# Transformer layer with attention and a mixture of experts on one core: the eight experts as one block, indirect transfers one at a time, and extra products ahead of the routing step

## The reference, cut to what matters

```python
xn = layernorm(x)                                   # x: 8 batches x 512 tokens x 128 channels
x  = x + attention(xn) + moe(xn)
# attention: 16 heads of width 8, keys where xn[..., 0] == 0 are masked
scores = einsum('bthd,bshd->bhts', q, k) * 8 ** -0.5;  attn = softmax(scores)
out    = einsum('bhts,bshd->bthd', attn, v) @ wo.T + bo
# moe: 8 experts, each of the 4096 tokens goes to its top 2, at most 1280 tokens an expert
logits = xt @ gate_w;  top_logits, top_idx = top_k(logits, 2)
rank   = cumsum(one_hot(top_idx)) - 1;  keep = rank < 1280
h      = gelu(exp_batches @ c_fc + fc_bias)         # exp_batches: 8 x 1280 x 128, h: 8 x 1280 x 512
y      = h @ c_proj + proj_bias
out    = sum over the two experts of weight * y[expert, rank]
```

## Time and profile before

| | us |
|---|---|
| median of 3 runs | 838.06 (835.35 to 841.63) |
| the profiled execution | 828.99 |
| its span, first to last instruction | 826.8 |
| PE busy | 614.4 (74%) |
| DVE busy | 410.8 (50%) |
| ACT busy | 403.2 (49%) |
| POOL busy | 220.1 (27%) |
| mean granted TensorE clock | 0.812 of full |

### The profile page before, as it was taken

The page is one execution under the profiler, slowest core; times in us unless marked ns, Lnnn a source line. Parts: engine busy times, 40 slices in busy tenths (PEclk is TensorE's granted clock), DMA queues, the critical chain, the costliest instruction groups (busy, mean ns, idle before and its releaser), DMA issues.

```text
span 826.8 us, 9722 instructions
## 1 busy us (share of the span) xinstructions
PE 614.4 (74%) x3502; PEld 306.7 (37%) x3502; DVE 410.8 (50%) x617; ACT 403.2 (49%) x781; POOL 220.1 (27%) x222
## 2 busy tenths in 40 slices
PE   5648997101399999899989999999989510269985
PEld 3423322000133333693358535863477100022322
DVE  6758676000278888317841685158713210045742
ACT  3340365000267777637883578457745200135761
POOL 3865128777200002000010002000200777740000
PEclk9975578555579999999999999999999655555975
DMA  7883341111101014112411232111312211100011
GB/s 199 254 261 115 128 160 61 51 51 51 39 22 41 28 35 131 33 33 73 122 41 33 69 95 73 33 53 48 104 44 72 72 51 51 50 22 22 2 52 51
DMA packets 57999, 60.44 MB, mean 73 GB/s; under 512 B 8032, under 2 KB 42848, under 8 KB 57952
## 3 DMA queue, kind: packets, MB, share of 16 engines
q1 hardware_dynamic: 52160, 45.92, 18.3%
q0 software_dynamic: 5792, 13.90, 5.4%
HBM read 29.65 MB, written 29.62 MB: 72 GB/s over the span
## 4 chain that ended last, share of the span: by engine, by line
PE 52%; another core or an unknown queue 13%; DVE 13%; ACT 10%; issue 6%; SPq 3%; DMA 3%; DVEq 0%; ACTq 0%
PE bX L933 14%; PE bPV L949 14%; PE bD L1039 9%; DVE nmax L731 8%; ACT probs L585 5%; PE bD L914 4%; ACT hid L615 2%; PE bX L923 2%; DMA k_rows<-hid 2%; PE bPV L1072 2%; PE bX L1024 2%; PE bX L1028 1%; PE bX L1025 1%; PE bD L968 1%
## 5 line engine op out<-in xcount | busy, mean ns | idle before, releaser
L731 DVE TENSOR_REDUCE nmax<-bD 128x2 f32<-128x1024 f32 x256 | 301.1, 1219 | 226.4 <-remote 147.7
L585 ACT ACTIVATE probs<-bX 128x512 f32<-128x512 f32 x512 | 269.4, 597 | 249.0 <-PE bX L933 110.0
L933 PE MATMUL bX<-Q,K 27*128 27x512 f32 x512 | 196.6, 519 | 133.4 <-issue 98.8
L933 PEld LDWEIGHTS bX<-Q,K 27*128 27x128 f32 x512 | 79.2, 202 | 291.0 <-issue 146.9
L949 PE MATMUL bPV<-probs,v_aug 128*32 128x512 f32 x1024 | 158.1, 693 | 1.6 <-ACT probs L585 0.7
L914 PE MATMUL bD<-K,Q 25*128 25x512 f32 x512 | 143.5, 529 | 14.8 <-issue 4.7
L487 POOL TENSOR_TENSOR wfc_hi<-wfc,ones 128x512 fp32r<-128x512 f32 x8 | 10.2, 1275 | 355.2 <-DMA pjb<-in_pjb 355.2
L1039 PE MATMUL bD<-wpj,hid 128*128 128x128 f32 x640 | 74.0, 276 | 7.7 <-DVE xeT_lo L764 4.8
L914 PEld LDWEIGHTS bD<-K,Q 25*128 25x128 f32 x512 | 60.7, 206 | 50.3 <-DVE nmax L731 23.3
L1039 PEld LDWEIGHTS bD<-wpj,hid 128*128 128x128 f32 x640 | 72.4, 192 | 9.4 <-issue 9.4
L615 ACT ACTIVATE hid<-bX,fcb 128x512 f32<-128x512 f32 (+1 forms) x96 | 55.2, 615 | 27.4 <-PE bX L1028 26.6
(11 more groups left out here) (103 smaller groups left out, 462.6 us busy)
## 6 DMA issues: line engine op xcount, KB each, us to landing
K<-k_rows SPq DMA_DIRECT2D x128, 50.0 KB
Q<-q_rows SPq DMA_DIRECT2D x128, 48.0 KB
slot_x<-hid POOLq DMA_DIRECT2D x10, 512.0 KB, 2.9
xe<-slot_x SPq DMA_DIRECT2D x8, 640.0 KB, 4.8
slot_y<-ye SPq DMA_DIRECT2D x8, 640.0 KB, 3.7
q_rows<-hid SPq DMA_DIRECT2D x8, 512.0 KB, 3.5
k_rows<-hid SPq DMA_DIRECT2D x8, 512.0 KB, 5.1
acc<-in_x SPq DMA_DIRECT2D x8, 256.0 KB, 5.1
```

The source lines that it names most:

```text
L585: taken(nc.scalar.activation(probs[:, (g % 2) * 4 + i, :], next_x()[:], ACT.Exp, scale=SCALE))
L731: nc.vector.tensor_reduce(nmax[q][:, k, 2 * pair:2 * pair + 2], bank()[:], AX.X, ALU.max, negate=True).then_inc(s_dd, 1)
L933: filled(nc.tensor.matmul(next_x()[:], K[u][rows_used, q, j * P:(j + 1) * P], Q[u][rows_used, q, :], start=True, stop=True))
```

## The change

All eight experts become one block that stands after batch 3 and the first four groups of batch 4 (68 groups done, 60 to come), with the rows of the next expert turned between the results of the one before, all the way through. The bias on `acc` is added before the zeroing and not after it, and the zeroing no longer waits for `s_nq`. Each of the 64 scatters waits until all ahead of it have landed; each gather waits for those of its batch, while the first gather of a batch is issued without a wait. GpSimd combines four batches instead of two, each after the third gather of the next batch; VectorE combines batches 4, 5 and 6 after groups 105, 112 and 119, and batch 7 at the end. SP writes the output of batches 0 to 3 during batches 6 and 7. On TensorE six full float32 products of 512 columns stand before the routing products, which no one reads, and the run-up has three `keep_clock` products a step in place of two.

```diff
@@ -58,17 +58,21 @@
 CH = [(0, 512), (512, 512), (1024, 256)]
 NCH = len(CH)
 KN = TOPK * NT
-EXPERTS_FROM, EXPERTS_TO = 2, 6
-assert 2 * (EXPERTS_TO - EXPERTS_FROM) == E
-COMBINED_BY_POOL = 2
+EXPERTS_AFTER = 3
+COMBINED_BY_POOL = 4
 N_CONST, N_LATER = 8, 3
...
+D_EXPERTS_FROM = D_FIRST + EXPERTS_AFTER * D_TURN + D_TURN
+
+
+GROUPS_BEFORE = (EXPERTS_AFTER + 1) * GB + 4
+
+
+COMBINED_AT = {GROUPS_BEFORE + 9 + 7 * b: b for b in range(COMBINED_BY_POOL, B - 1)}
...
@@ -337,34 +352,36 @@
             def load_rows(e):
                 sp.dma_start(xe[:], slot_x_v[e]).then_inc(s_xe, 16)
 
-            def load_experts(b):
-
-                e = b * 2 - 2 * EXPERTS_FROM
+            def load_expert(e):
+                q = e % 2
+                sp.dma_start(wfc[q][:], c_fc[e]).then_inc(s_w[q], 16)
+                sp.dma_start(wpj[q][:], c_pj_v[e]).then_inc(s_w[q], 16)
+                sp.dma_start(fcb_s[q][:], fcb[e]).then_inc(s_w[q], 16)
+                sp.dma_start(pjb_s[q][:], pjb[e].to_broadcast([P, C])).then_inc(s_w[q], 16)
+
+            def experts():
                 sp.wait_ge(s_put, KN * 16)
...
-                before = (b - EXPERTS_FROM) * (D_TURN + D_EXPERTS) + D_EXPERTS_FROM
-                sp.wait_ge(s_dd, before + NCH)
-                load_rows(e0 + 1)
-                for q in range(2):
-                    sp.wait_ge(s_dd, before + (3 + q) * NCH)
-                    sp.dma_start(slot_y_v[e0 + q], ye[:]).then_inc(s_slot, 16)
+                load_rows(0)
+                for e in range(E):
+                    if e < E - 1:
+                        sp.wait_ge(s_dd, rows_item(e, NCH - 1) + 1)
+                        load_rows(e + 1)
+                    sp.wait_ge(s_dd, results_end(e))
+                    sp.dma_start(slot_y_v[e], ye[:]).then_inc(s_slot, 16)
+                    if e + 2 < E:
+                        load_expert(e + 2)
 
...
@@ -376,21 +393,27 @@
                 load_quad(b + 1, 1, 0)
                 max_rows(0, 0, m + 2)
                 if with_experts:
-                    load_experts(b)
+                    for e in range(2):
+                        load_expert(e)
                 sp.wait_ge(s_x, x_filled(b, 15))
                 load_quad(b + 1, 1, 1)
                 max_rows(0, 1, m + 3)
                 if with_experts:
-                    experts(b)
+                    experts()
+
+            def put_out(b):
+                sp.dma_start(rows(out_v, b), rows(acc, b)).then_inc(s_out, 16)
+
+            def take_pool(start, stop):
+                for b in range(start, stop):
+                    sp.wait_ge(s_comb_p, b + 1)
+                    put_out(b)
 
             each_turn(turn)
 
-            for b in (*range(COMBINED_BY_POOL, B - 1), *range(COMBINED_BY_POOL), B - 1):
-                if b < COMBINED_BY_POOL:
-                    sp.wait_ge(s_comb_p, b + 1)
-                else:
-                    sp.wait_ge(s_comb, b + 1 - COMBINED_BY_POOL)
-                sp.dma_start(rows(out_v, b), rows(acc, b)).then_inc(s_out, 16)
+            for b in range(COMBINED_BY_POOL, B):
+                sp.wait_ge(s_comb, b + 1 - COMBINED_BY_POOL)
+                put_out(b)
             sp.wait_ge(s_out, B * 16)
 
 
...
@@ -465,41 +488,32 @@
                 pool.wait_ge(s_wr[b], WR_DMAS * 16)
             per = SLOTS * C // P // ZERO_DMAS
             nc.gpsimd.memset(hid_f[:, 0:per], 0.0).then_inc(s_fill, 1)
+            pool.wait_ge(s_xn, B)
+            nc.gpsimd.tensor_tensor(acc[:], acc[:], bo_s[:, None, :].to_broadcast([P, NT, C]), ALU.add).then_inc(s_bo, 1)
             pool.wait_ge(s_fill, 7)
-            pool.wait_ge(s_nq[0], MAX_DMAS * 16)
             for h in range(ZERO_DMAS):
                 pool.dma_start(slot_x.rearrange("(p h r) c -> h p (r c)", p=P, h=ZERO_DMAS)[h], hid_f[:, 0:per]
                                ).then_inc(s_zero, 16)
                 pool.wait_ge(s_zero, h * 16 + 16)
-            nc.gpsimd.tensor_tensor(acc[:], acc[:], bo_s[:, None, :].to_broadcast([P, NT, C]), ALU.add).then_inc(s_bo, 1)
-            pool.wait_ge(s_xn, B)
             for k in range(TOPK):
                 for n in range(NT):
                     col = k * NT + n
+                    wait(pool, s_put, col * 16)
                     pool.indirect_dma_start(slot_x, bass.IndirectOffsetOnAxis(ap=put_i[:, col:col + 1], axis=0),
                                             xn_all[:, n, :], None, bounds_check=SLOTS - 1, oob_is_err=False
                                             ).then_inc(s_put, 16)
-            for b in range(EXPERTS_FROM, EXPERTS_TO):
-                for q in range(2):
-                    steps_before = (b * 2 - 2 * EXPERTS_FROM + q) * 2
-                    pool.wait_ge(s_w[q], b * 64 - (EXPERTS_FROM - 1) * 64)
-                    wide = "p (h c) -> p h c"
-                    nc.gpsimd.tensor_tensor(wfc_parts[q][0][:].rearrange(wide, c=P), wfc[q][:].rearrange(wide, c=P),
-                                            ones[:, None, :].to_broadcast([P, HC, P]), ALU.mult).then_inc(s_split, 1)
-                    pool.wait_ge(s_split, steps_before + 1)
-                    nc.gpsimd.tensor_tensor(wfc_parts[q][1][:], wfc[q][:], wfc_parts[q][0][:].bitcast(F32), ALU.subtract
-                                            ).then_inc(s_split, 1)
-            pool.wait_ge(s_slot, E * 16 + 16)
-            for b in range(B):
-                for k in range(TOPK):
-                    for n in range(TT):
-                        col = k * NT + b * TT + n
-                        pool.indirect_dma_start(gathered(b, k * TT + n), None, slot_y,
-                                                bass.IndirectOffsetOnAxis(ap=get_i[:, col:col + 1], axis=0),
-                                                bounds_check=SLOTS - 1, oob_is_err=False).then_inc(s_get[b], 16)
-            for b in range(B):
+            for e in range(E):
+                q = e % 2
+                pool.wait_ge(s_w[q], e // 2 * 64 + 64)
+                wide = "p (h c) -> p h c"
+                nc.gpsimd.tensor_tensor(wfc_parts[q][0][:].rearrange(wide, c=P), wfc[q][:].rearrange(wide, c=P),
+                                        ones[:, None, :].to_broadcast([P, HC, P]), ALU.mult).then_inc(s_split, 1)
+                pool.wait_ge(s_split, e * 2 + 1)
+                nc.gpsimd.tensor_tensor(wfc_parts[q][1][:], wfc[q][:], wfc_parts[q][0][:].bitcast(F32), ALU.subtract
+                                        ).then_inc(s_split, 1)
+
+            def combine(b):
                 pool.wait_ge(s_get[b], TOPK * TT * 16)
-            for b in range(COMBINED_BY_POOL):
                 got = xn_all[:, b * TOPK * TT:(b + 1) * TOPK * TT, :].rearrange("p (k n) c -> p k n c", k=TOPK)
                 weights = wgt[:].rearrange("p (k n) -> p k n", k=TOPK)[:, :, b * TT:(b + 1) * TT]
                 for k in range(TOPK):
@@ -508,6 +522,18 @@
                 link(last)
                 link(nc.gpsimd.tensor_tensor(rows(acc, b), rows(acc, b), got[:, 0], ALU.add))
                 nc.gpsimd.tensor_tensor(rows(acc, b), rows(acc, b), got[:, 1], ALU.add).then_inc(s_comb_p, 1)
+
+            pool.wait_ge(s_slot, E * 16 + 16)
+            for b in range(B):
+                for k in range(TOPK):
+                    for n in range(TT):
+                        col = k * NT + b * TT + n
+                        wait(pool, s_get[b], (k * TT + n) * 16)
+                        pool.indirect_dma_start(gathered(b, k * TT + n), None, slot_y,
+                                                bass.IndirectOffsetOnAxis(ap=get_i[:, col:col + 1], axis=0),
+                                                bounds_check=SLOTS - 1, oob_is_err=False).then_inc(s_get[b], 16)
+                        if 0 < b <= COMBINED_BY_POOL and (k, n) == (0, 2):
+                            combine(b - 1)
 
 
         @block.scalar
...
@@ -809,6 +834,8 @@
                     take_out(b - 1)
                 if g == GROUPS + 1:
                     normalise(0)
+                if b * GB + g in COMBINED_AT:
+                    combine(COMBINED_AT[b * GB + g])
 
             scores_max(0)
 
@@ -829,19 +856,16 @@
             def turn(b, with_experts, last):
                 for g in range(4, GB):
                     group(b, g, last)
-                    if last and g >= GB - 4:
-                        combine(g - GB + 4 + COMBINED_BY_POOL)
                 if last:
+                    dve.wait_ge(s_dd, d.value())
                     normalise(1)
-                    combine(B - 2)
                     take_out(b)
-                    dve.wait_ge(s_dd, d.value())
                     combine(B - 1)
                     return
                 for g in range(4):
                     group(b + 1, g)
                 if with_experts:
-                    experts(b)
+                    experts()
 
             each_turn(turn)
 
...
+                up(E - 1, chunks)
                 for c in range(NCH):
-                    down(e0 + 1, 1, c)
```

(7 more changed lines are left out.)

93 lines of the change are left out of this document (46 added, 47 removed).

## The result

The changed kernel takes 781.87 us (median of 4, 779.45 to 785.29) beside 839.85 for the kernel before (4 runs, 835.35 to 865.56): ratio 0.933 [0.927, 0.939], faster, as forecast in sign. The size is missed by far: 782 where 666 stood, outside the range of 642 to 710.

The account below looks back on a forecast made before the run. Unawaited indirect transfers were taken to stall the engines, 178 us lost. Group 68 at 286.0 + 14 wait and half clock + 157 experts + 142 + 7 + 2 + 55.6 tail = 663.6, plus 2.2 outside: 666; range 642 to 710.

Parts of the forecast that it names:

- What bounds the kernel: Under scatter and gather, runs of unawaited indirect transfers stall all engines but GpSimd, losing 87 and 91 us, 178 together.
- rival 3: The stall has another cause than transfers in a row and stays as long: 828 us, no change; chance 0.03.
- The scatter: On GpSimd, 64 awaited scatters at 2.6 us each, issue plus landing, take 166.4 us and end at 288.6.
- the 14 of wait and half clock: Before the experts, TensorE waits 7.4 us for the first rows and loses 7 restarting at half clock.
- The front: Before group 0, six products cost about 1 us and keep the clock up; group 0 starts at 85.0, not 92.5.
- The 8.5 that should have been won: In the run-up, 13 steps at full clock go from 1.88 us to 1.23 each, saving 8.5 us.
- rival 1: In the front, the six products don't hold the clock; group 0 at about 99, whole 673 us; chance 0.16.
- The experts: The block of eight takes 157 us, about 19.4 an expert, with loads of weights and rows hidden behind the work.
- After the experts: Groups 142 us, VectorE's combinations +7, wait for batch 4's gather +2, tail 55.6; a batch's gather 19.5, GpSimd's combination 3.0.
- +7 at 2.74: At batch 4's combination, the wait for the gather is 7 us instead of 2 if a transfer takes 2.74 us.
- rival 2: Under scatter and gather, the stall is only halved, each transfer still holding the engines up: 739 us; chance 0.09.
- rival 4: The stall lasts while any indirect transfer is under way, 264 of 322 us lost: 914 us, slower; chance 0.05.

Follow-up runs that it names:

- Experiment 1: The changed kernel with its indirect transfers issued without waits, 699.8 us; and the kernel before, unchanged, run once more for its trace, 683.82 us.
- experiment 2: The changed kernel, unchanged, run beside the kernel before on one chip: 783.76 us beside 670.83 us.
- rows first: The changed kernel with SP asking for the rows of expert e + 2 before it waits for the results of expert e: 748.57 us.

## Why the prediction was right or wrong

**What bounds the kernel.** Right for the trace that it read, and wrong as a rule. The group shows the stall, and that it coincides with unawaited transfers; from one trace the prediction concluded that such a run of transfers sets it off. Experiment 1 shows the same transfers without it. (One reading is also off: when the value products at 133.89 began, three transfers had been issued and not four, and TensorE's first pause comes behind 136.6.) What stands: in the two comparisons where the kernel before stalled, awaited transfers did not. That awaiting is what cures it is not shown, since no unawaited form of the new order ran in those surroundings, so of the 0.933 only the 782 is explained here. The Trainium skill ("SBUF — State Buffer", Who interferes with whom) says that a DMA never contends with a compute engine; the trace without the stall agrees with it (83.15 of 86 us busy under 61 scatters); in the stalled one (15.35 of 86) it is open whether the transfers held anything up. So rival 3 named a real possibility, a cause outside the transfers' own cost, though its time of 828 did not come.

**The scatter.** This is the step that failed first. Issue plus landing was the right form, but its size was not: 2.6 us a transfer was taken, between 2.25 and 3.4, from the 2.74 in the earlier trace rows; it is 3.04 alone, 3.45 beneath groups and 3.35 in the mean. The last gather of a back-to-back run is no awaited one: it landed 1.74 us behind the end of its issue, an awaited gather takes 2.33 there and a scatter 2.06. Why it is less in such a run is not shown. The prediction even took 0.14 off the 2.74, where something was to be added. By the Trainium skill ("DMA: Bandwidth & Descriptors", Anatomy of one DMA) 2.0 us plus the bytes over 436 GB/s makes an estimate of 2.15 us for 64 KB. The wait of 2.06 behind each issue agrees with it; the spacing does not, since the 0.97 of issuing comes on top. Halving the bytes took off 0.09. And the scatter began at 126.1 and not 122.2, behind ten zeroings of 3.7 in place of 3.37. Its end moved from 288.6 to 339.7, when SP asks for the first rows, and TensorE's wait from 7.4 to 49.6. Against the 14 of wait and half clock that stood in the sum this is +35.6; the half clock that really followed lies in the block.

**The front.** Right that the clock would be full beneath the scatter, wrong on where: it fell at about 66.5 us, some 3 us after the last of the six products, when TensorE had begun to wait for VectorE (0.44 and 0.63 us idle before the steps at 64.83 and 65.97), and the run-up went at 2.30 us a step, three fillers at half clock, to 89 us. The 8.5 that should have been won were lost (+8.8). That is rival 1's mechanism, as far as the clock goes, and luck has a part in it: in the trace of experiment 2 the same kernel had group 0 at 86.60. It has no consequence for the time, since the scatter set the start of the block: 782.19 there, 781.86 here, and 783.12 without the six products.

**The experts.** TensorE's work was right to a per cent: 156.3 us measured with rows first, 157 predicted. The word "hidden" for the rows was wrong. This is the second step that failed. The prediction priced their landing (4.8, now 6.3) but not their place in SP's queue, behind a wait for results, a store and four loads of weights: +35.8.

**After the experts.** VectorE asked for batch 4 at 650.5, 113.3 after the block, where 112.4 stood. The batch was there 146.1 after it and not 114.3: a gather takes 3.33 and more, so a batch with its share of combining takes 27.9 ((682.06 - 542.45) / 5, by GpSimd's timeline), where 19.5 and 3.0 stood. Of the +36.1 the wait is 30.8, and most of the other 5.3 goes with the clock behind it (0.59 from 683 to 726 us). That part is not owed to the wait alone: with two in flight and no wait the last batch still took 6 more than 47.3 + 7. The prediction had the mechanism and its sensitivity (+7 at 2.74), and the size of one number wrong; it is the same number as for the scatter.

**Rivals and range.** None of the rivals' times came: no stall was left (rival 2), and no group was held up by single transfers (rival 4: 82.91 of 86 busy). All three misses are of one sign, and two hang on the same price. At 3.0 us the prediction itself gave 706. Worked the same way, 3.35 a scatter adds 64 x 0.75 = 48, 3.33 for each of the 40 gathers to batch 4 adds 29, and the late rows add 36: 779 as an estimate, beside 782 measured. The path through the kernel was right; one price and one wait in a queue were not.

## What to carry to other kernels

An awaited indirect transfer costs issue plus landing, not the larger of the two. Take the landing from a transfer that was awaited, not from the last of an unawaited run, count both times the number of transfers, and see whether the work that covers them is longer. Two in flight gave back nearly all of it (654.38 us at the lowest, 653.77 without waits, 744.96 with one in flight). When a step is called hidden, follow the queue it is issued from to what stands ahead of it there, since a load that lands in 6 us can be asked for 10 us late. And take a second trace, elsewhere, before a change is built on something in the first that no instruction explains.

The version with two transfers in flight and rows first takes 661 to 674 us (medians of three comparisons), 0.84 of the changed kernel in the comparison that had both (660.99 / 783.76). It is within some 2% of the kernel before where that does not stall (lowest times 654.38 to 647.62, 654.12 to 650.02, 662.57 to 648.32), so no gain over it is shown. Where that does stall, it has not run.

## What the runs showed of the hardware

- The kernel before has two times, 648 to 688 us and 829 to 866 us. In the trace of the second TensorE, VectorE and ScalarE begin instructions late under both runs of unawaited indirect transfers (VectorE by up to 34.5 and 46.7 us), 147.7 us of it on VectorE put down to no releaser. The two times came on one chip. Their cause is open.
- An awaited scatter of 128 rows comes 3.04 us behind the last with 512 bytes a row, and 2.95 with 256; unawaited they come 1.28 apart, with two in flight 1.73 in the mean. The landing alone is 2.06 behind the issue for a scatter and 2.33 for a gather.
- The clock of the front differs between executions with the same instructions there. The changed kernel had 0.50 from 69 to 88 us in one trace and 0.87 in another; from 88 to 136 us it was at 0.98 or more in nine traces and at 0.50 to 0.58 in six.
